# A four-layer graph network: node tables inside the first edge loop, weighted one-hots on GpSimd, nine record slots, straight step code, early last-layer strips

## The reference, cut to what matters

```
layer 0:  fwd = relu(relu([x_dst, x_src, ea16] W1f + b1f) W2f + b2f)   summed over dst
          bwd = relu(relu([x_src, x_dst, ea16] W1b + b1b) W2b + b2b)   summed over src
          out = relu(relu([fwd_sum, bwd_sum] W1n + b1n) W2n + b2n)
layer 1:  per edge a small MLP of ea8 (8 -> 64 -> 64 -> 256) gives four 8x8 weights;
          messages of x_src, ea4 and these weights, summed over dst; plus h Ws, h Wv
layer 2:  10 times  h = 0.9 * norm * segment_sum((h * norm)[src], dst) + 0.1 * feat
layer 3:   3 times  X = segment_sum(edge_weight * X[dst], src)
```

## Time and profile before

| | us |
|---|---|
| median of 3 runs (2962.78 to 2967.89) | 2966.73 |
| profiled execution, its own time | 2968.53 |
| its span, first to last instruction | 2966.7 |
| busy: PE, DVE, ACT, POOL | 2367.7, 1951.6, 1175.8, 1336.7 |

### The profile page before, as it was taken

How to read it: one execution, slowest core, us unless ns; L and a number is a source line. 1 busy time by engine, 2 the same in 40 slices (tenths; PEclk the granted TensorE clock), 3 DMA queues, 4 the chain that set the end, 5 groups by cost and what they waited for, 6 DMA issues and landing times. The chain is left out here.

```text
span 2966.7 us, 73733 instructions
## 1 busy us (share of the span) xinstructions
PE 2367.7 (80%) x27993; PEld 1705.4 (57%) x27993; DVE 1951.6 (66%) x4960; ACT 1175.8 (40%) x2507; POOL 1336.7 (45%) x1688
## 2 busy tenths in 40 slices
PE   0439879889249999999999958888988769995695
PEld 0214333333127888888888835565656569995474
DVE  5815444444169999999999937988989744443001
ACT  1014333333105555555555527777878600000010
POOL 2017777777704555555555506766767500000000
PEclk9957675655559999999999968999989979997897
DMA  8964444444302343334333316767666330003966
GB/s 355 365 243 112 114 113 113 113 115 111 99 21 66 120 147 113 112 114 154 112 111 134 124 50 190 187 169 187 171 178 173 93 78 3 3 3 157 399 246 250
DMA packets 251434, 424.13 MB, mean 143 GB/s; under 512 B 127586, under 2 KB 213244, under 8 KB 241747
## 3 DMA queue, kind: packets, MB, share of 16 engines
q1 hardware_dynamic: 195124, 334.25, 31.8%
q0 software_dynamic: 54800, 83.75, 11.7%
q10 hardware_dynamic: 1164, 1.37, 0.1%
HBM read 229.60 MB, written 209.72 MB: 148 GB/s over the span
## 5 line engine op out<-in xcount | busy, mean ns | idle before, releaser
L330 POOL DMA_INDIRECT sorted_edges<-s_records,s_index x400 | 476.3, 1191 | 313.3 <-issue 308.8
L1543 PE MATMUL m_p_acc<-m_prod,m_oh 128*128 128x344 f32 x1250 | 432.2, 492 | 1.5 <-DVE m_prod L1604 1.5
L1082 DVE TENSOR_SCALAR e_ohw<-e_iota,e_rec 128x128 bf16<-128x128 f32 x628 | 400.0, 695 | 0.0
L866 POOL TENSOR_TENSOR e_ohw<-e_oh,e_rec 128x512 bf16<-128x512 bf16 x314 | 332.3, 1078 | 76.3 <-DVE e_oh L1074 76.1
L1543 PEld LDWEIGHTS m_p_acc<-m_prod,m_oh 128*128 128x128 f32 x1250 | 243.7, 206 | 110.2 <-issue 27.1
L872 POOL TENSOR_TENSOR e_part<-e_rest,e_part 128x256 bf16<-128x256 f32 x157 | 103.7, 661 | 401.4 <-ACT e_part L902 399.0
L1585 DVE TENSOR_TENSOR m_prod<-m_rec,m_coef 128x256 f32<-128x256 f32 x471 | 232.2, 544 | 0.0
L1796 PE MATMUL q_p_next<-q_g,A 128*128 128x96 bf16 x5250 | 224.8, 206 | 0.0
L1796 PEld LDWEIGHTS q_p_next<-q_g,A 128*128 128x128 bf16 x5250 | 223.7, 98 | 0.0
L1096 DVE COPY e_strip<-e_p_aw 128x512 f32<-128x512 f32 (+1 forms) x325 | 199.8, 654 | 1.5 <-PE e_p_aw L974 1.4
L893 ACT ACTIVATE e_hid<-e_p_hid,e_b 128x512 f32<-128x512 f32 x157 | 107.9, 687 | 221.8 <-PE e_p_hid L958 221.8
(11 more groups left out here) (347 smaller groups left out, 5021.6 us busy)
## 6 DMA issues: line engine op xcount, KB each, us to landing
dense_strips<-e_strip SPq DMA_DIRECT2D x25, 3200.0 KB, 11.1
r_W<-dense_strips SPq DMA_DIRECT2D x47, 1600.0 KB, 24.7
m_rec<-sorted_edges SPq DMA_DIRECT2D x138, 526.0 KB, 3.8
sorted_edges<-s_neg SPq DMA_DIRECT2D x5, 12560.0 KB, 68.4
A<-dense_strips POOLq DMA_DIRECT2D x25, 800.0 KB, 8.0
e_rec<-sorted_edges SPq DMA_DIRECT2D x156, 108.0 KB, 2.2
sorted_edges<-s_records,s_index POOLq DMA_INDIRECT x400, 3.9
m_rec<-sorted_edges SPq DMA_DIRECT2D x12, 394.5 KB, 3.7
```

What stands on the lines that cost most here:

```text
L330: pool.indirect_dma_start(dram["edges"], bass.IndirectOffsetOnAxis(ap=index[u % RING][:, c:c + 1], axis=0), record[u % RING][:, c, :], Non ...
L866: i = g_.tensor_tensor(ohw[g % 4][:, :, k, :], oh[s][:, :, 0, :], rec[s][:, :, c:c + 1].to_broadcast([P, G, P]), ALU.mult)
L1082: i = V.tensor_scalar(ohw[g % 4][:, t, 0, :], iota[:, :], rec[s][:, t, CSRC:CSRC + 1], rec[s][:, t, CW:CW + 1], ALU.is_equal, ALU.mult)
L1543: i = mm(p_acc[d % 2][:, 0:TERMS], oh[g % 4][:, t % G, :], prod[g % 3][:, t % G, :], start=(t % NB == 0), stop=(t % NB == NB - 1), skip_gr ...
```

## The change

- `load_nodes_phase` goes. Its work stands in `layer0_edges_phase`: x comes already turned as an input (`x_turned`), 13 tables of two blocks are multiplied by TensorE, cut by ScalarE (high and middle), VectorE (subtraction) and GpSimd (low). ScalarE issues the 18 weight transfers that SyncE issued.
- First loop: `weigh_hi` goes, GpSimd makes all three weighted one-hots. The bias matmul goes; VectorE adds the bias in PSUM (`add_bias`), and ScalarE's `relu2` waits for that. The three matmuls of the source sum are one of 99 columns, and `copy_from` adds the parts. Its sum has a PSUM bank of its own.
- Spilled tiles: the wait for the strips' stores stands behind the records' load.
- Node phases: layernorm in two parts, of 16 and 9 blocks.
- Layer one: nine record slots.
- Layer two: straight code; the last step has the source block as its outer loop, and after each two source blocks SyncE loads a last-layer strip into the SBUF of their counts. Thirteen (HELD) buffers in the last layer.

```diff
-        @block.sync                                   # load_nodes_phase, removed
-            ...
+            sp.dma_start(xT[:, :], io["x_turned"]).then_inc(n_load, 16)
...
+            for i in range(TABLES):                   # GpSimd
+                n, to, _ = table(i)
+                tab_mid.after(pool, i)
+                tab_low.set_by(g_.tensor_tensor(to[:, :, 2, :], tab_rest[i % 2][:, 0:n, :], to[:, :, 1, :], ALU.subtract))
...
-                for k, c in ((1, CR), (2, CL)):
+                for k, c in ((0, CW), (1, CR), (2, CL)):
                     i = g_.tensor_tensor(ohw[g % 4][:, :, k, :], oh[s][:, :, 0, :], rec[s][:, :, c:c + 1].to_broadcast([P, G, P]), ALU.mult)
...
+            for i in range(TABLES + 1):               # ScalarE, after its 18 transfers
+                if i < TABLES:
+                    n, to, y = table(i)
+                    tabled.after(act, i)
+                    tab_hi.set_by(nc.scalar.copy(to[:, :, 0, :], y))
+                if i:
+                    n, to, _ = table(i - 1)
+                    tab_cut.after(act, i - 1)
+                    tab_mid.set_by(nc.scalar.copy(to[:, :, 1, :], tab_rest[(i - 1) % 2][:, 0:n, :]))
...
+            for i in range(TABLES):                   # VectorE
+                n, to, y = table(i)
+                tab_hi.after(dve, i)
+                tab_low.before(dve, i, 2)
+                dve.sem_inc(prime, 1)
+                tab_cut.set_by(V.tensor_tensor(tab_rest[i % 2][:, 0:n, :], y, to[:, :, 0, :], ALU.subtract))
...
-                mm(p_flow, ones3[:, :], b2s[:, :], start=True, stop=False, skip_group_check=True)
...
+            def add_bias(g):
+                flow_done.after(dve, g)
+                biased.set_by(V.tensor_tensor(p_flow, p_flow, b2[:, :, :, :].rearrange("p t k h -> p t (k h)"), ALU.add))
...
-                staged(j, (copy_dense, 1), (copy_from, 0), (weigh_hi, 4), (one_hots, 7), (cut_rest, 3))
+                staged(j, (copy_dense, 1), (copy_from, 0), (one_hots, 7), (add_bias, 3), (cut_rest, 3))
...
-        SLOTS = 6
+        SLOTS = 9
...
+                for k in range(HELD):                 # layer two, SyncE
+                    released.after(sp, min(2 * k + 1, NB - 1))
+                    bring_strip(sp, dram, keep["pair"], k, k)
...
-                with pe.Fori(1, STEPS2 // U + 1) as n:
+                for u in range(STEPS2 - 1):
...
+                last = STEPS2 - 1
+                for b in range(NB):
+                    if b % 4 == 0:
+                        gathered[b // 4].after(pe, last - 1)
+                    for d in range(NB):
+                        m = nc.tensor.matmul(p_last[d // BANK][:, d % BANK, :], A[b][:, d * P:(d + 1) * P], g3[last % 2][:, b, :, :],
+                                             start=(b == 0 and d % BANK == 0), stop=(b == NB - 1), skip_group_check=True)
+                    released.set_by(m)
```

More of the change, by code:

```diff
@@ L607, in set_by @@
         instruction.then_inc(self.semaphore, 1)
[L610 to L631, removed]
-        @block.sync
[L634 to L682, removed]
@@ L918, in _ @@
             mm = nc.tensor.matmul
+            pe.wait_ge(n_load, 80)
+            for i in range(TABLES):
+                n, _, y = table(i)
+                tab_cut.before(pe, i, 3)
+                for k in range(n):
+                    m = mm(y[:, k, :], xT[:, (2 * i + k) * P:(2 * i + k + 1) * P], wsd[:, :, :].rearrange("p k h -> p (k h)"), start=True, stop=True,
+                           skip_group_check=True)
+                tabled.set_by(m)
             pe.wait_ge(d_b, 288)
-            pe.wait_ge(d_w, 16 * 9)
+            pe.wait_ge(d_w, 16 * 6)
             pe.wait_ge(setup, 2)
-            pe.wait_ge(cleared, 2)
+            pe.wait_ge(cleared, 4)
             def turn(g):
@@ new lines, in product @@
+                def product(u, c, d, b):
+                    at = (4 * c + d) * P
+                    return nc.tensor.matmul(p_s[c][:, d, :], A[b][:, at:at + P], g3[u % 2][:, b, :, :], start=(b == 0), stop=(b == NB - 1),
+                                            skip_group_check=True)
+                for u in range(STEPS2 - 1):
+                    for b in range(NB):
+                        if u and b % 4 == 0:
+                            gathered[b // 4].after(pe, u - 1)
+                        for d in range(width[0]):
+                            m = product(u, 0, d, b)
+                    summed[0].set_by(m)
+                    for c in range(1, CH):
+                        if c >= 4:
+                            gathered[c - 3].after(pe, u)
+                        for d in range(width[c]):
+                            for b in range(NB):
+                                m = product(u, c, d, b)
+                        summed[c].set_by(m)
@@ L2059, in _ @@
             sp.dma_start(stacked[:, :], io["sort_consts"][:, 3, 0:D]).then_inc(d_stacked, 16)
-            for free, b, k in loads:
-                if free:
-                    sp.wait_ge(summed, free)
-                sp.dma_start(W[k][:, :, :].rearrange("p d c -> p (d c)"), dram["strips"][b, :, 1, :]).then_inc(arrived[k], 16)
+            large = sp.value_load(keep["large"][0:1, 0:1], min_val=0, max_val=1)
+            with sp.If(large):
+                for k in range(HELD):
+                    bring_strip(sp, dram, keep["pair"], k, k)
+            for free, b, k in loads[HELD:]:
+                sp.wait_ge(summed, free)
+                bring_strip(sp, dram, keep["pair"], b, k)
             sp.wait_ge(final, 1)
```

281 lines of the change are left out of this document (136 added, 145 removed).

## The result

The changed kernel takes 2827.3 us in the median of four runs (2823.0 to 2829.0); the kernel before took 2966.5 beside it. The ratio is 0.953 (95% interval 0.9514 to 0.9547). Forecast: 2818, range 2790 to 2855. The profiled run took 2829.0 us, its span is 2827.2.

What follows compares the result with a forecast made beforehand. VectorE and TensorE both full in the first loop, record stalls in layer one, strip waits in the last layer's first step. Terms -33 -10 -7 -50 -49 = -149 us on 2966.7 gave 2818 us, range 2790 to 2855.

Steps and rivals of the forecast that it cites:

- Ahead of the first loop: Before the first loop: tables and weight loads become one phase, TensorE starts at about 855.5, 33 us sooner.
- the ring of two: Tables ahead of the first loop: two remainder places close a subtract, cast, subtract chain, 2.9 us for two tables.
- First loop: First loop: VectorE loses four weighted one-hots and gains the bias; mean period 5.24 to 5.17 us, -10 us.
- The chain of the earlier trace: First loop: TensorE's turn waits for an earlier remainder in a shared PSUM bank; period 5.13 us without a VectorE limit.
- the hidden bias: First loop: VectorE's bias step, 0.42 us, ends before the one-hot copy lets relu2 start, so it adds nothing.
- VectorE's sum: First loop before the change: VectorE's work was taken as the period, 5.17 us, falling to 3.4 us after.
- slack before turn: First loop: TensorE's idle time ahead of turn, where nine fewer matmuls of fused sums and bias were said to lie.
- Rival (a): First loop: GpSimd's one-hot products collide more than once a group, period 5.6 us, kernel 2880 us; chance 0.10.
- Spilled tile and node phases: Spilled tiles: work runs under the store's wait, -5 us; layer zero's node phase -2, layer one's 0; together -7 us.
- Layer one: Layer one's loop: nine record slots in place of six remove 18 stalls of 2.78 us, -50 us.
- Layer two and last layer: Straight code saves 18.5 us; early strips shorten the last layer's first step to 56 us; together -49 us.
- rival (d): Early strips delay instruction fetches and the phase change by 15 us, or come late: up to 2865 us; chance 0.08.

Runs made afterwards that it cites:

- e10_tables: Changed kernel with nine of ScalarE's eighteen weight transfers issued by SyncE and three table-remainder places in place of two: 2821.3 us, ratio 0.9522.
- e4_no_bias: Changed kernel without the first loop's bias addition, leaving the second layer's bias out: 2822.7 us, ratio 0.9529.
- e2_before_hi_on_gpsimd: Kernel before with only one part of the change, all weighted one-hots of the first loop by GpSimd: 2958.4 us, ratio 0.9989.
- e7_spill_queue: Changed kernel with the spilled records fetched from ScalarE's queue in place of SyncE's: 2824.2 us, ratio 0.9503.
- e3_six_slots: Changed kernel with six record slots in layer one in place of nine: 2873.7 us, ratio 0.970.
- e11_best: Changed kernel with reordered first loop, dense split around second, early stacked constant, weight issues shared with SyncE and three remainder places: 2787.9 us, ratio 0.9405.
- e9_order2: Changed kernel with a second new order of TensorE's and ScalarE's steps in the first loop, same work: 2789.9 us, ratio 0.943.
- e12_pieces: Version of e11_best with each block's strip stored in five 640 KB transfers in place of one of 3.2 MB: 2733.9 us, ratio 0.9212.

## Why the prediction was right, and where not

- **Ahead of the first loop, -33, measured -28.7.** A mis-sized term: ScalarE's eighteen issues took 14.8 us, 0.82 each, not 10. And a wrong mechanism that cost nothing: 1.45 us a table by the ring of two. It was 1.71 by TensorE at half clock (e10_tables): the sum priced ScalarE, VectorE and GpSimd and put TensorE at nothing, though the earlier trace rows had its 33 us of work.
- **First loop, -10, measured -9.5.** The chain of the earlier trace rows, the hidden bias and GpSimd's fit are as written (period 5.16; e4_no_bias). Wrong is the reason: I named VectorE's sum as what set 5.17 before, and the chain as second. TensorE's own work was a third bound at the same 5.16, and e2_before_hi_on_gpsimd shows that the move alone gains nothing that can be measured. What misled me is in the earlier trace rows: that iteration is the fourth, when the pipeline is still filling, and TensorE does no sums in it. Later they add 0.6 us of matmuls to each, the 0.61 us that TensorE stood at 907.10, so the "slack before turn" was not there. The sums in the kernel before, 903 to 1711 us:

```profile
L1003 PE MATMUL e_p_to<-e_part,e_oh 128*128 128x33 bf16 x1848 | 70.6, 178 | 0.5 <-issue 0.5
L1010 PE MATMUL e_p_to<-e_part,e_oh 128*128 128x33 bf16 x1848 | 70.5, 178 | 0.1
```

  That the forecast held is in part luck: a bound that it did not have was lifted by an edit to which it gave no worth. The bias matmul that goes (0.21 us), the fused sums (0.12) and what follows them took TensorE's work from 5.13 to 4.66 us a group; the bias needs VectorE's room (with the one-hots back on VectorE, +165 us); and the cycle then keeps 5.155.
- **Rival (a), GpSimd clocks the loop:** it had 0.58 us a group to spare (91.2 of 817 us idle). The 4.1 us for three products, with the collision's price, was right (4.04).
- **Spilled tile and node phases, -7, measured -4.2.** The records were to land under the store's wait; they land with the store (e7_spill_queue), so the compute behind them stays outside. From the last strip's store to the tile's last store it is 17.9 us in place of 20.1, -2.2 where 5 were forecast; the node phases gave the 2 forecast.
- **Layer one, -50, measured -49.8 to P2** (the loop alone -52.0), by the term as written (e3_six_slots). It is now VectorE's: 514 of 520 us.
- **Layer two and last layer, -49, measured -45.1.** Straight code: the last step of layer two begins at P2+241.5 in place of P2+260.4, -18.9 (forecast -18.5), and the thirteenth strip is there at P2+297.9 (298). TensorE's start P2+299, measured P2+298.1, gated by the small transfer as written. The first step is mis-sized: 56 us forecast as bound by transfers, 61 measured, bound by TensorE: 53.7 us of work (25 strips at the 1.98 us that most of them take would be 49.5) and 7 us of waits for instructions, for which the sum had nothing in this step (rival (d), at half its price). Second step +1.7, third with what follows it +4.6 (forecast 0 and +6).

## What to carry to other kernels

Before a load is taken off a full engine, count every bound of the loop on its own, each engine's sum and each cycle through a shared buffer: three stood within 0.02 us here (VectorE 5.17, TensorE 5.16, the cycle 5.155), and lifting the first alone gave nothing that can be measured. Take the rows for this from the middle of a loop, not from where it fills. Then the order of steps inside an iteration is worth as much as the work: with the same work it gave 5.74, 5.16 and 4.96 us. When the compute bound is gone, look at what a large transfer does to small ones and to instruction fetch; here cutting it into pieces was worth 54 us.

## What the runs showed of the hardware

- A 3.2 MB store delays the landing of a small load to its own landing even from another engine's queue (VectorE goes on 10.0 us after the store's issue, both ways; with the store done, in the kernel before, such a load landed in 1.7 us).
- Straight code too waits for instructions while the transfer engines are full: up to 3.1 us at a time and 35 us in all in e11_best's first loop, 7 us in six places of the last layer's first step. In the loops of e9_order2 and of the changed kernel, with the same 3.2 MB stores, TensorE's longest stand between 885 us and the last group is 0.5 and 0.9 us; what they have and e11_best lacks is a wait of TensorE, 0.3 and 0.5 us, in each iteration. That this wait is what hides the fetch is not shown. The Trainium skill (page "Runtime: NRT & Kernel Launch", "Instruction fetch mechanics") calls the fetch of straight code mostly hidden; here that held where transfers left room (share 0.45 to 0.55 in e12_pieces) and in those two loops, and not in e11_best.
- Behind such a pause TensorE's granted clock fell from 1.00 to 0.79 in the mean of 8 us. It fell to the lower level behind eleven of the 15 pauses of e11_best and behind all three of e2_before_hi_on_gpsimd, the shortest of them 1.3 us. In the loops of the changed kernel, e9_order2 and e12_pieces, where no pause is over 1.2 us, it stayed at 1.00 from 885 us on, though TensorE stands 0.5 us in each iteration of the first. Why four pauses, of 1.8 to 2.6 us, had no such fall is open.
